# Two-layer transformer step on one core: experts and second normalisation in one block, first experts' weights loaded earlier

## What is computed

```
xn = layernorm(x)
s  = attention_like(xn)            # layer 0: linear recurrence; layer 1: causal attention, 16 heads
g  = silu(mixture_of_experts(xn))  # layer 0: 16 experts + shared expert; layer 1: 8 experts, top 2
x  = x + s * g
```

## Time and profile before

| | us |
|---|---|
| median of three runs | 2626.52 (2626.50 to 2628.46) |
| the profiled execution's own time | 2629.02 |
| its span, first to last instruction | 2627.2 |
| PE busy in the span | 2461.7 (94%) |
| experts: first up projection to last output scaled | 405.5 to 766.9 |
| renormalize: first Silu to the end of its block | 787.9 to 850.3 |

### The profile page before, as it was taken

One profiled execution on the slowest core, in us unless ns is written; L12 is line 12 of the kernel. 1 busy time (PEld: TensorE's weight loads), 2 busy tenths in 40 slices (PEclk: granted clock), 3 DMA queues, 4 the chain that ended last, 5 costly groups with the idle time before them and its releaser, 6 DMA issues. The chain is left out here.

```text
span 2627.2 us, 45420 instructions
## 1 busy us (share of the span) xinstructions
PE 2461.7 (94%) x14584; PEld 1698.8 (65%) x14585; DVE 1298.9 (49%) x3186; ACT 1115.7 (42%) x2580; POOL 554.5 (21%) x510
## 2 busy tenths in 40 slices
PE   6999998999965899999999999999999998999993
PEld 5555554555535566666666666666666668999993
DVE  5766231212217765555656566556565653333334
ACT  3211111111115466666666666666666663222222
POOL 3002002444326233332111111111111110111113
PEclk9999998999987899999999999999999999999997
DMA  6012105865436223332111211112212115666696
GB/s 207 17 48 64 48 32 161 260 195 158 105 79 208 81 81 97 99 101 65 41 40 40 56 48 40 45 34 56 65 49 56 48 53 208 241 239 240 237 338 224
DMA packets 145780, 295.78 MB, mean 113 GB/s; under 512 B 16816, under 2 KB 102720, under 8 KB 135328
## 3 DMA queue, kind: packets, MB, share of 16 engines
q1 hardware_dynamic: 124752, 251.79, 29.8%
q0 software_dynamic: 20944, 42.94, 6.1%
HBM read 194.00 MB, written 67.12 MB: 99 GB/s over the span
## 5 line engine op out<-in xcount | busy, mean ns | idle before, releaser
L1634 DVE CUSTOM_DVE_ANT_0 at_p<-at_ps,atk_mask 128x640 f32<-128x640 f32 (+7 forms) x512 | 375.8, 754 | 250.5 <-PE at_ps L1414 140.9
L1467 ACT ACTIVATE at_p<-at_p,at_nmax 128x640 f32<-128x640 f32 (+7 forms) x512 | 391.6, 769 | 64.9 <-DVE at_nmax L1634 61.5
L1474 ACT ACTIVATE at_pT<-at_ps 128x512 f32<-128x512 f32 (+1 forms) x640 | 327.2, 555 | 213.7 <-PE at_ps L1414 210.4
L1502 POOL TENSOR_TENSOR at_qkT<-kept_xg 128x1024 f32<-128x1024 f32 x64 | 150.8, 2357 | 1038.6 <-DVE kept_xg L1651 1038.6
L1414 PEld LDWEIGHTS at_ps<-atk_ident,at_p 128*128 128x128 f32 x2304 | 255.5, 141 | 147.1 <-issue 126.5
L1666 DVE SCALAR_TENSOR_TENSOR late_y<-at_ps,at_inv,late_y 128x256 f32<-128x256 f32 x512 | 215.2, 478 | 227.1 <-PE at_ps L1441 195.1
L1414 PE MATMUL at_ps<-atk_ident,at_p 128*128 128x128 f32 x2304 | 317.1, 278 | 9.0 <-ACT at_pT L1474 4.0
L1404 PE MATMUL at_ps<-at_qkT 64*128 64x512 f32 (+3 forms) x1536 | 293.8, 501 | 7.4 <-DVE at_nmax L1634 4.3
L1431 PE MATMUL at_ps<-at_pT,at_v 128*64 128x256 f32 (+1 forms) x2560 | 277.9, 363 | 0.0
L1386 PE MATMUL at_ps<-atk_h,atk_w 128*128 128x512 f32 x512 | 243.1, 598 | 6.5 <-SPq L1257 6.5
L1431 PEld LDWEIGHTS at_ps<-at_pT,at_v 128*64 128x64 f32 x2560 | 172.7, 137 | 99.5 <-issue 21.8
(11 more groups left out here) (236 smaller groups left out, 3227.9 us busy)
## 6 DMA issues: line engine op xcount, KB each, us to landing
moe_w<-in_w_w SPq DMA_DIRECT2D x53, 1028.0 KB
kept_xg<-kept_xg SPq DMA_DIRECT2D x256, 128.0 KB
atk_first_w<-in_w_w SPq DMA_DIRECT2D x18, 1028.0 KB
atk_w<-in_w_qkv SPq DMA_DIRECT2D x32, 384.0 KB, 3.0
slot_in<-ex_zero SPq DMA_DIRECT2D x9, 1032.0 KB
ex_wg<-in_w_eg SPq DMA_DIRECT2D x16, 512.0 KB
ex_wu<-in_w_eu SPq DMA_DIRECT2D x16, 512.0 KB
ex_wd<-in_w_ed SPq DMA_DIRECT2D x16, 512.0 KB
```

What stands on the lines that cost most here:

```text
L1467: act.activation(buf, buf, ACT.Exp, bias=nmax[:, unit:unit + 1], scale=-1.0, accum_out=rsum[:, unit:unit + 1]).then_inc(exp_done, 1)
L1474: act.activation(dst, ring[RING_BANK[part][ev]][:, 0:(i1 - i0) * P].rearrange("p (k c) -> p k c", c=P), ACT.Copy).then_inc(t_read, 1)
L1502: pool.tensor_tensor(out=qkT[x][:, :].rearrange("p (m t) -> p m t", m=2)[:, :, half * CH:(half + 1) * CH], in0=raw[half][:, :].rearrange(" ...
L1634: dve.tensor_tensor_reduce(out=p[unit % LAG][:, 0:(n[0] + 1) * P], in0=scores(*n), in1=mask[:, T - (n[0] + 1) * P:T], scale=-1.0, scalar=3 ...
```

## The change

1. `experts` and `renormalize` become one stage. `renormalize` no longer opens a scope and a block; it returns five functions, one per engine, which are appended to the streams of `experts`. Their bodies are those of before (the tile `turned` is now a pair of half tiles). The normalised chunks `stage` are written into the experts' gate and up weight buffers, `scaled` into their down weight buffers, `turned` into `hid`.
2. At the head of the second part ACT waits for the last gelu and runs a Silu of one column (`warm`).
3. The weights of experts 0 and 1 are loaded by SP in `first_layer` after its second pair of chunks, into columns of the transposed activations of sequences 0 and 1, which are used up by then; the experts' other tiles lie in used-up columns too. SP's loop over four pairs becomes two loops over two.
4. One identity `d.at_ident`, loaded in `normalize`, serves all stages; the other three loads of it and PE's wait for it in `experts` go.
5. The big tile of the transposed activations is kept to the end: `moe_w2`, `at_y`, `moe_ya` and, in attention, `qkT` and `y_stage` are slices of it.

The diff, cut to its core:

```diff
@@ normalize
-        ident = s.sb("ident", P)
+        ident = d.at_ident
@@ renormalize
-def renormalize(nc, d):
-    with ExitStack() as ctx:
-        s = Scope(nc, "n1", ctx)
...
-        stage = [s.sb(f"stage{j}", GT * C) for j in range(4)]
-        scaled = [s.sb(f"scaled{u}", GT * C) for u in range(2)]
-        turned = [s.sb(f"turned{u}", KC * CH) for u in range(2)]
...
-        s.start()
-        with nc.Block() as block:
...
+def renormalize(d, s, ps, gel, gel_done, stage, scaled, turned):
...
+    warm = s.sb("warm", 1)
...
+    def scalar(act):
...
+        act.wait_ge(gel_done, KF * E0 + ONE)
+        act.activation(warm[:, :], gel[0][:, 0:1], ACT.Silu)
+        for g in range(4):
+            squash(g)
...
+    return sync, vector, gpsimd, tensor, scalar
@@ first_layer, SP
-                with sp.Fori(0, HB) as i:
+                def chunks(i):
                     for u in range(2):
...
+                with sp.Fori(0, HB // 2) as i:
+                    chunks(i)
+                for u in range(2):
+                    for dst, src in zip(d.ex_w[u], (d.w["eg"], d.w["eu"], d.w["ed"])):
+                        sp.dma_start(dst, src[u * P:(u + 1) * P, :]).then_inc(d.ex_w_in[u], 16)
+                with sp.Fori(HB // 2, HB) as i:
+                    chunks(i)
@@ experts
-        wg, wu, wd = ([s.sb(f"{n}{u}", w) for u in range(2)] for n, w in (("wg", KC * F0), ("wu", KC * F0), ("wd", KF * C)))
-        ident = s.sb("ident", P)
+        wg, wu, wd = ([d.ex_w[u][j] for u in range(2)] for j in range(3))
+        ident = d.at_ident
...
+        second = renormalize(d, s, ps, gel, gel_done, wg + wu, wd, [hid[0:2], hid[2:4]])
+        then = dict(zip(("sync", "vector", "gpsimd", "tensor", "scalar"), second))
         s.start()
         with nc.Block() as block:
             @block.sync
             def _(sp):
-                sp.dma_start(ident[:, :], d.ident).then_inc(consts, 16)
...
                 sp.dma_start(spare[:, :], d.spare).then_inc(spare_in, 16)
-                for u in range(2):
-                    load(u, u)
...
                     sp.dma_start(tiles(d.n1_z[g][:, :]), rows_of(d.z, g)).then_inc(d.n1_z_in[g], 16)
+                then["sync"](sp)
...
                     scatter(e, e % 2, False)
+                then["gpsimd"](pool)
...
-                pe.wait_ge(consts, 16 + ONE)
                 turn(0, 0)
...
@@ attention
-        qkT = [s.sb(f"qkT{u}", 2 * T) for u in range(2)]
+        qkT = [d.moe_ya[:, TB * C + u * 2 * T:TB * C + (u + 1) * 2 * T] for u in range(2)]
...
-        y, y_stage = d.at_y, s.sb("y_stage", TB * C)
+        y, y_stage = d.at_y, d.moe_ya[:, 0:TB * C]
@@ build
+        big = k.sb("big", 2 * KC * N)
+        d.xnT, d.hT = big[:, 0:KC * N], big[:, KC * N:2 * KC * N]
...
+        d.at_ident = k.sb("ident", P)
...
+        d.ex_w = [[piece(n) for n in at] for at in ((0, 1, 3), (4, 5, 6))]
...
                 experts(nc, d)
-                renormalize(nc, d)
```

More of the change, by code:

```diff
@@ L915, in experts @@
         AHEAD = 4
-        wg, wu, wd = ([s.sb(f"{n}{u}", w) for u in range(2)] for n, w in (("wg", KC * F0), ("wu", KC * F0), ("wd", KF * C)))
-        ident = s.sb("ident", P)
+        wg, wu, wd = ([d.ex_w[u][j] for u in range(2)] for j in range(3))
+        ident = d.at_ident
         rows = d.ex_rows
         xg = d.xg
-        xT = [[s.sb(f"xT{u}{c}", B * CAP) for c in range(KC)] for u in range(2)]
-        gel = [s.sb(f"gel{j}", B * CAP) for j in range(2)]
-        hid = [s.sb(f"hid{f}", B * CAP) for f in range(KF)]
-        eo = [s.sb("eo0", B * C), d.ex_eo]
-        zero, spare = s.sb("zero", TB * ROW), s.sb("spare", TB)
+        xT, gel, hid = d.ex_xT, d.ex_gel, d.ex_hid
+        eo = [d.ex_eo0, d.ex_eo]
+        zero, spare = d.ex_zero, s.sb("spare", TB)
         ps = s.banks()
@@ L1052, in _ @@
                 expert(ROUNDS - 1, AHEAD - 1, lambda: None)
+                then["tensor"](pe)
             @block.scalar
@@ L1073, in _ @@
                 gelus(E0 - 1)
+                then["scalar"](act)
             @block.vector
@@ L1093, in _ @@
                                               d.slot_w[:, ds(b * E0 + e, 1)], None, ALU.mult).then_inc(eo_done, 1)
+                then["vector"](dve)
 RING = 3
@@ L1926, in build, with piece @@
         d.xg = [k.sb(f"xg{q}", B * C) for q in range(4)]
-        d.gathered = k.sems("gathered", 4, software=True)
+        d.gathered, d.ex_w_in = k.sems("gathered", 4, software=True), k.sems("w_in")
+        big = k.sb("big", 2 * KC * N)
+        d.xnT, d.hT = big[:, 0:KC * N], big[:, KC * N:2 * KC * N]
+        d.moe_w2, d.at_y, d.moe_ya = big[:, 0:E1 * KH * C], big[:, E1 * KH * C:E1 * KH * C + TB * C], big[:, E1 * KH * C + TB * C:E1 * KH * C + NT * C]
+        d.at_ident = k.sb("ident", P)
+        def piece(n):
+            b, c, of = n // (2 * KC), n // 2 % KC, n % 2
+            return (d.xnT, d.hT)[of][:, c * N + b * T:c * N + (b + 1) * T]
+        d.ex_w = [[piece(n) for n in at] for at in ((0, 1, 3), (4, 5, 6))]
+        d.ex_xT = [[piece(n)[:, c * CH:(c + 1) * CH] for c in range(KC)] for n in (7, 9)]
+        d.ex_gel = [piece(10)[:, j * CH:(j + 1) * CH] for j in range(2)]
+        d.ex_hid = [piece(n)[:, f * CH:(f + 1) * CH] for n in (11, 13) for f in range(2)]
+        d.ex_eo0, d.ex_zero = piece(14), d.xnT[:, 2 * T:2 * T + TB * ROW]
         k.start()
```

434 lines of the change are left out of this document (212 added, 222 removed).

## The result

The changed kernel takes **2611.2 us** in the median (2609.4 to 2616.3, five runs), the kernel before 2626.8 beside it: ratio 0.9943, 95% interval 0.993 to 0.9957. The forecast was 2611.2. Two later comparisons gave 0.9949 [0.9935, 0.9962] and 0.9951 [0.9937, 0.9964]. The profiled execution took 2612.5 us, its span 2610.7.

The account below looks back on a forecast made before the run. PE, busy 94% of the span, bounds the kernel, so gains lie at two seams: 11.8 + 3.6 - 0.1 = 15.3 us, taking the median from 2626.5 to 2611.2 us; range 2606.5 to 2616.

Parts of the forecast that it names:

- Part 1: Seam from experts to second normalisation: one stage instead of two removes POOL's drain and the barrier, gain 11.8 us.
- list of signs: At the same seam: DVE's first multiply about 10 us after the experts' last output is scaled, not 22.
- in-time argument for the later chunks: In the second normalisation: z's second chunk is squashed 1 us before it is due, the last lands some 10 us early.
- Part 2: Start of the experts: starting all the merged stage's semaphores there delays PE by 0.6 us (bounds 0.3 and 1.0).
- Part 3: Start of the experts: identity and weights at hand let PE project sooner, gain 3.6 us with the 0.6 counted in.
- Rival B: First layer: the early weights disturb PE there, costing up to 7.6 us, 2618.8; chance 0.04.
- the weights alone "would give 2.9 less": Start of the experts: early weights without the resident identity would give 2.9 us less.
- The clock: Start of the experts: PE's half-speed stretch taken as unchanged; bounds a gain of 2.75 us and a loss of 0.7.
- Rival A: Seam after the experts: POOL is not free when its issues end, chain loses up to 3.0 us, 2613.2; chance 0.12.
- the rival's sign: For Rival A: POOL's first root no sooner than 19 us behind the experts' last output, not 15; chance 0.12.
- Rival E: Attention: `qkT`'s new home slows 1536 score matmuls; 10 ns each would cost 15.4 us; chance 0.02 for more.

Follow-up runs that it names:

- e3: The kernel before, its boundary kept, but with no drain of POOL at the end of the experts' block: ratio 0.9962.
- e1: The changed kernel with the second half of the merged stage in a block of its own again, in the same scope: ratio 0.9982.
- e7: The changed kernel with an explicit drain of POOL between its last scatter and its part of the normalisation: ratio 0.9944.
- e5: The kernel before, with the last expert's four scatters each waiting for its own sequence's output: ratio 0.9978.
- e8: The kernel before, its boundary kept, with the four loads of z moved behind the boundary: ratio 0.9998.
- e4: The changed kernel, with the last expert's four scatters each waiting for its own sequence's output: ratio 0.9922.
- e2: The changed kernel with the weights of experts 0 and 1 loaded at the head of the experts again, the identity still resident: ratio 0.9955.
- e6: The changed kernel without the one-column Silu and its wait: ratio 0.9948.
- e10: The same kernel as e4, against the kernel before on another chip: 2610.0 us, ratio 0.9933.

## Why the prediction was right

Against its own steps:

- **Part 1, forecast 11.8, measured 11.74.** z's first load landed 4.6 us behind its issue (4.5 taken), the multiply came 11.29 us behind the scaling; the prediction's sum had 11.2 (777.2 - 765.98), its list of signs "about 10". e3 and e1 show the cause: the drain 9.9, the rest of the boundary 1.8. The in-time argument for the later chunks held as well; chunk 0's stage began 8.90 us behind the multiply, as before (797.90 - 789.01 = 8.89).
- **Part 2, forecast 0.6, measured about 1.0.** The barrier is passed 1.2 us later, 0.24 of which the first layer was late already. This term was mis-sized: 0.13 us for an increment was read from four of them at another stage's start, here eight fill 1.4 us (397.5 to 398.9), and in the kernel before the four at this same place already filled 1.0 (396.7 to 397.7).
- **Part 3, forecast 3.6 net, measured 3.34** from the first layer's end, 3.10 on the clock. PE started 0.2 us behind its barrier, not the 0.5 taken, which gave back most of what part 2 took too little. The early weights cost nothing that shows: the first layer is 0.24 us later at its end, and its store at 226.86, ahead of them, was so by 0.11; their six issues took 3.9 us of SP's time and not 2.7. Rival B is out. One remark of this part is wrong, though nothing hangs on it: that the weights alone "would give 2.9 less". ACT was done at 402.60 and PE waited until 405.51, so by those rows they would give 2.9; that was not run by itself.
- **The clock.** Taken as unchanged, and no effect of the change on it is shown: the low stretch of the profiled pair was 2 us shorter and the experts took 1.02 us less, but a second execution of the changed kernel has 5.8 us and 360.55, about as before. It was inside the bound of 2.75.
- **Rival A** was a true mechanism for a drain, and not for this change: e7 puts the drain in, POOL's first root comes 19.7 us behind the last scaling, as the rival's sign had it, and the first chunk is 1.7 us later; the changed kernel has 16.0 us and no drain.
- **Rival E.** The scores' matmul takes the same time from its new home, by the group by line (busy us, mean ns):

```profile
L1406 PE MATMUL at_ps<-kept_big 64*128 64x512 f32 (+3 forms) x1536 | 293.7, 501 | 7.7 <-DVE at_nmax L1636 4.6 <-POOL kept_big L1504 3.0
```

- **The total was right to 0.1 us by some luck.** The two seams gave 15.1 us (15.3 forecast), and their shares repeated in all three profiled executions of the changed kernel. The rest of what was measured is the 1.02 us of the experts, which come and go, and what lies behind attention's start, where the forecast had nothing. The profiled pair differs there by -2.34 in attention and +1.5 at the end. The latter is mostly TensorE's clock at the start of the last stage: the same 32 matmuls took 5.25 us before and 6.51 after, at a granted 0.71 and 0.57; the twelve other executions took 5.41 to 6.01.
- **Attention is the open point.** On the two chips where kernels of both kinds were profiled, it took 1328.4 to 1330.0 us in the three that keep the old homes of tiles (e3, e5, e8) and 1331.8 to 1333.0 in the five with the new ones; the first pair shows the opposite, 1332.4 before and 1330.1 after. So the new homes may cost some 3 us there, which would be rival E at 2 ns for each score matmul; the rows do not single them out (their mean on these chips is 500 to 503 ns with the new home, 500 to 501 with the old), and giving `qkT` its old home back was not tried. The ratios of the change, 0.9943, 0.9949 and 0.9951, are 15.0, 13.4 and 12.9 us. The last two fall short of the seams' 15.1, as such a cost would have it, but on the chip where the changed kernel was not timed nothing is short: there e4 is 20.3 us faster than the kernel before and e2 11.8, and with the 4 us of the split scatters taken off and the 4.6 of the early weights put on, both come to about 16, an estimate. The gain is better told as 13 to 16 us than as 15.6.

## What to carry to other kernels

Where a stage ends in indirect or accumulating transfers issued by GpSimd, look at the row of its drain at the stage's end, and not at the engines' busy time: here it holds all five engines for 10 us, though the next stage begins with rows that need only the first of those transfers, and merging the next stage into the same block removes it, because GpSimd goes on with its next work behind its last issue. What remains behind such a seam is the wait for the data itself; there it paid to let each transfer wait for its own input (4 us) more than to tidy semaphores (0.4 us) or tables (nothing). A gain at a seam is best proved at the seam, by the distance between two instructions that both kernels have: it repeated to 0.1 us in three executions of the changed kernel, where totals moved by several.

## What the runs showed of the hardware that was not expected

- GpSimd's drain ends 4.5 to 4.7 us behind the landing of its last transfer, in five kernels, with and without other loads in flight; with such loads beside it the landing itself moves from 3.8 to between 7.1 and 8.1 us.
- A table load is not held by the wait of the activation that it belongs to: it ran 18 us ahead of it (755.88 and 774.16 in e6).
- One and the same kernel (e4 and e10) spent 11.4 us less in attention on one chip than on another, 1321.4 against 1332.8, while attention begins at 834.56 and 834.38. PE's busy time accounts for 4.9 of it and its idle time for 6.5. The reason is open; the four kernels profiled on the faster chip all took 1320.5 to 1321.7. Without the kernel before beside it on the same chip, e4 would have seemed 10 us better than it is.
